# Attention on one Trainium2 core: the values product of a 512-query step in one piece instead of two

## The reference, cut to what matters

```
def _attn(x, wq, wk, wv, wo, bq, bk, bv, bo):
    q, k, v = ...                               # 16 heads of 8 dimensions
    att = jnp.einsum('bhqd,bhkd->bhqk', q, k) * hd ** (-0.5)
    att = jnp.where(causal, att, -jnp.inf)
    att = jax.nn.softmax(att, axis=-1)
    y = jnp.einsum('bhqk,bhkd->bhqd', att, v)
    return y.transpose(...).reshape(Bb, T, C) @ wo + bo
```

## Time and profile before

| | us |
|---|---|
| median of 3 runs | 3347.49 (3345.98 to 3355.19) |
| the profiled execution | 3349.13 |
| its span in the profile | 3347.4 |
| the 512-query groups 4 to 7 of one causal layer | 73.2 |
| all 24 groups of one causal layer, 903 to 1275 | 372 |

### The profile page before, as it was taken

One profiled execution on the slowest core, in us unless ns is written; L12 is line 12 of the kernel. 1 busy time (PEld: TensorE's weight loads), 2 busy tenths in 40 slices (PEclk: granted clock), 3 DMA queues, 4 the chain that ended last, 5 costly groups with the idle time before them and its releaser, 6 DMA issues. The chain is left out here.

```text
span 3347.4 us, 75365 instructions
## 1 busy us (share of the span) xinstructions
PE 2748.5 (82%) x29824; PEld 1299.9 (39%) x29824; DVE 2337.0 (70%) x3203; ACT 2171.7 (65%) x4160; POOL 331.7 (10%) x868
## 2 busy tenths in 40 slices
PE   4459999699499994859999998389996996799967
PEld 3322332599333332612222222233333995233326
DVE  5659997322499993469999996499993223799953
ACT  1137889354278983339999998168884453588853
POOL 3023110000031100000000000031100000221000
PEclk8669999799699997969999999699997998799988
DMA  2060000000500001140000000600001003200010
GB/s 56 7 142 27 13 11 8 30 0 0 126 21 15 10 10 45 40 88 8 10 8 10 8 8 25 138 18 16 12 10 32 1 0 75 65 18 11 10 34 25
DMA packets 96737, 99.80 MB, mean 30 GB/s; under 512 B 13158, under 2 KB 84644, under 8 KB 96420
## 3 DMA queue, kind: packets, MB, share of 16 engines
q1 hardware_dynamic: 79140, 77.62, 8.8%
q10 hardware_dynamic: 16640, 15.73, 1.9%
q0 software_dynamic: 640, 2.10, 0.2%
HBM read 51.44 MB, written 43.65 MB: 28 GB/s over the span
## 5 line engine op out<-in xcount | busy, mean ns | idle before, releaser
L1189 ACT ACTIVATE h_probsf<-h_ps_scoresf 128x512 f32<-128x512 f32 (+3 forms) x1216 | 603.5, 552 | 155.3 <-PE h_ps_scoresf L1141 142.9
L1189 ACT ACTIVATE h_probsg<-h_ps_scoresg 128x512 f32<-128x512 f32 (+3 forms) x1216 | 603.6, 552 | 150.8 <-PE h_ps_scoresg L1141 138.3
L1189 ACT ACTIVATE h_probsb<-h_ps_scoresb 128x512 f32<-128x512 f32 x1024 | 556.3, 596 | 73.8 <-PE h_ps_scoresb L1141 63.8
L1163 PE MATMUL h_ps_valuesf<-h_probsf,v_all 128*9 128x256 f32 (+2 forms) x4608 | 348.8, 375 | 29.5 <-POOL h_probsf L1252 21.9
L1163 PE MATMUL h_ps_valuesg<-h_probsg,v_all 128*9 128x256 f32 (+2 forms) x4608 | 347.5, 374 | 26.3 <-POOL h_probsg L1252 18.6
L1163 PE MATMUL h_ps_valuesb<-h_probsb,v_all 128*9 128x256 f32 x4096 | 318.4, 383 | 9.4 <-ACT h_drainedb L1196 4.8
L1212 DVE TENSOR_REDUCE h_maxima_0b<-h_ps_scanb 128x2 f32<-128x1024 f32 x256 | 292.5, 1217 | 10.9 <-PE h_ps_scanb L1103 9.6
L1212 DVE TENSOR_REDUCE h_maxima_2b<-h_ps_scanb 128x2 f32<-128x1024 f32 x256 | 292.8, 1217 | 6.7 <-PE h_ps_scanb L1103 6.7
L1103 PE MATMUL h_ps_scanf<-k_stack,q_stack 48*128 48x512 bf16 (+3 forms) x1280 | 218.1, 363 | 69.9 <-DVE h_ps_valuesf L1201 51.5
L1212 DVE TENSOR_REDUCE h_maxima_0f<-h_ps_scanf 128x2 f32<-128x1024 f32 x224 | 259.2, 1219 | 22.6 <-PE h_ps_scanf L1103 22.3
L1103 PE MATMUL h_ps_scang<-k_stack,q_stack 48*128 48x512 bf16 (+3 forms) x1280 | 217.0, 361 | 70.3 <-DVE h_ps_valuesg L1201 50.4
(11 more groups left out here) (423 smaller groups left out, 3865.9 us busy)
## 6 DMA issues: line engine op xcount, KB each, us to landing
q_stack<-q_parts ACTq DMA_DIRECT2D x20, 256.0 KB, 8.3
k_stack<-k_parts ACTq DMA_DIRECT2D x20, 256.0 KB, 9.8
q_stack<-q_parts SPq DMA_DIRECT2D x20, 256.0 KB, 8.8
k_stack<-k_parts SPq DMA_DIRECT2D x20, 256.0 KB, 10.7
attended<-h_drainedf SPq DMA_DIRECT2D x16, 256.0 KB, 2.3
attended<-h_drainedf SPq DMA_DIRECT2D x32, 128.0 KB, 1.9
attended<-h_drainedb SPq DMA_DIRECT2D x32, 128.0 KB, 1.9
attended<-h_drainedg SPq DMA_DIRECT2D x16, 256.0 KB, 2.2
```

Of the source, the lines that this page charges most:

```text
L1163: last = nc.tensor.matmul(ps_values[32 * j:32 * j + VD, low:high], m.v_all[:, kb, QUAD * quad + j, :], probs[:, (u + j % banks) % RING_P, ...
L1189: nc.scalar.activation(by_head(probs[:, of % RING_P, :], of), by_head(ps_scores[:, of % RING_S, :], of), ACT.Exp, scale=SOFTMAX_SCALE).the ...
```

## The change

`halves` gives one piece for every step, whatever its width:

```
@@ class Plan, def halves(self, n_step) @@
         high = self.queries(self.steps[n_step][0])
         width = high - self.offsets[n_step]
-        n = 2 if width > CH // 2 else 1
-        return [(high - width + h * width // n, high - width + (h + 1) * width // n) for h in range(n)]
+        return [(high - width, high)]
```

## The result

The changed kernel is slower: median 3401.12 us (3400.59 to 3407.52, four runs) against 3346.73 before, ratio 1.0162 with a 95% interval of 1.0141 to 1.0183. The forecast was 3383 with a range of 3340 to 3410. The direction and the mechanism were right, and the place in the main; the size was 54 us where I had 36. The 3401 measured lies nearer to the 3406 of the clock rival than to the forecast.

A forecast was written before the change was run, and what follows sets the result against it. PE, DVE and ACT's loop were taken to bound groups 4 to 7 together. Terms of 1.2, 3.0, 2.1, 0.4, 1.8 and 0.5 gave 9.0 us a layer, 36 in four: 3383 us (median), chance 0.60, range 3340 to 3410.

The forecast's parts named there:

- the clock rival: Thinner PE work makes the granted clock fall twice more a layer, 2.9 us each, +23 us: 3406 us; chance 0.12.
- Three limits within 6%: Groups 4 to 7 bound at once by ACT's loop 1.07, PE's cycle 1.09 and DVE's scan 1.13 us.
- The piece left, 1.00 us: One values piece of 512 columns holds PE 1.00 us, bounded by 0.90 and 1.12; ends worth -10 to +12 us.
- The spacing, 1.07 and 1.53 us, a step of 2.60: Plain-scan steps: score gap without values 1.07 us (ACT's loop), with values 1.53 (PE's work); step 2.60, before 2.18 or 2.27.
- Third scans: A second scan placed in the hole makes the next scan wait for DVE, up to 0.6 us; together +1.8 us a layer.
- Groups 4 to 7, 8.5 us a layer: Losses in groups 4 to 7 of each causal layer: 1.2, 3.0, 2.1, 0.4 and 1.8 us; 80 to 83 us for 73.2.
- The diagonal steps: Steps with diagonal scans go from 2.54 to 2.78 us, +0.24 on PE's terms; 5 of a group's 13 scans are diagonal.
- Groups 0 to 3, 0.5 us a layer: Group 0 loses nothing; groups 1 to 3 lose 3 x 0.35 x 0.5 = 0.5 us, part hidden by waits for scan buffers.
- Groups 8 to 23, 0: These groups keep their pieces and start from the same state, so they keep their time: 0.
- Faster through less PE work: Rival: 6.7 us a layer of PE work comes off, DVE caps it at 5.2, 21 in all: 3327 us; chance 0.13.
- DVE decides: Rival: both scans of a step fit the hole, group time is that of its scans, no change: 3350 us; chance 0.15.

The follow-up runs named there:

- the filled changed kernel: Changed kernel plus extra 0.22 us scans into a free buffer at the ends of groups 1 and 7 and the change from 22 to 23: 1.0114, median 3385.34 us.

## Why the prediction was right, and where its size was off

- *Three limits within 6%.* Borne out for ACT's loop: shorter exponentials gain the kernel before 0.28%. For DVE no run tested it in the kernel before.
- *The piece left, 1.00 us.* Measured 0.98. Its width costs nothing else (the run with two products in one turn).
- *The spacing, 1.07 and 1.53 us, a step of 2.60.* Measured 1.07 and 1.52, 2.59; shorter exponentials move the first to 0.86 and not the second.
- *Third scans.* They are there, with a wait of 0.47 us each. I had 1.8 us a layer. Without them (the old order with one piece) groups 5 and 6 are 0.5 and 0.6 us shorter at the full clock, and the kernel 0.3%, about 10 us or 2.6 a layer, part of which may be the clock.
- *Groups 4 to 7, 8.5 us a layer.* Measured 8.0 in the two profiled executions, and 9.0 with both kernels at the full clock. The two differ in group 4. I counted 1.2 us for it, and at the full clock it is 1.2 (19.6 against 18.4). The profiled executions show nothing (20.7 against 21.0) because the fall in group 4 lasts 3.4 us after the change in the two middle layers and 6.8 before: the changed kernel got back some 1.5 us there, which I had not foreseen. The diagonal steps had 0.4 to 0.5 a group; they cost nothing that shows in groups 4 and 5, and 0.7 each in groups 6 and 7.
- *Groups 0 to 3, 0.5 us a layer.* About right for the work: 0.7 at an unchanged clock (29.3 against 28.6), all in group 1. Groups 2 and 3 show none of it; in group 3, where DVE is busy 10.17 of 10.70 us, DVE would hide it whole and not by half, though no run tested that. The rest of the 1.9 to 3.3 us in the table is falls of the clock.
- *Groups 8 to 23, 0.* The orders are the same from group 8 on, as I said, but the layers lost 0.7 to 4.3 us to falls of the clock there, 8.4 in all. With those stretches filled all four take 247.2 at a clock of 1.00.
- *The clock rival* had 0.12, as a case apart. It came about together with the forecast. The step that failed is that I priced falls at 0 in the sum, though the row with a fall after 1.92 us of work in 3.40 stood beside a step that leaves PE idle a quarter of the time. By the filled changed kernel that term is 16 us: 38 for the work and 16 for the falls are the 54 measured. That the range held 3401 is owed to its width, and not to a price for the clock in the sum. The price I did name, 2.9 us a fall, was too high as well, since it compared group 4 with group 5: group 4 against itself without the fall is 21.0 against 18.4, 2.6.
- *Faster through less PE work:* PE's busy time did fall by 1.9 us in groups 4 to 7 (66.43 for 68.31) and the groups took longer all the same. *DVE decides:* refuted by groups 5 and 6 with shorter maxima, which fall by only 0.5 us each.

The 16 us are measured for the filled kernel as a whole. How they divide between layers was seen in one profiled execution only, and falls move between executions.

## What to carry to other kernels

When PE, DVE and ACT are within a few per cent of each other, as here, the length of PE's longest uninterrupted piece can matter more than the sum of its work. It has to fit inside the loop that feeds the next engine, here 1.07 us for a ring of three score banks, of which 0.53 is already spoken for by scores and scan. A piece of 256 columns (0.56 us) just fits, one of 512 (0.98) doesn't. Compare each piece with that loop, before counting what is saved on fixed costs. And a change that opens holes in PE's stream should be priced at both clock levels; a group whose clock differs between two profiles is compared at equal clock before its difference is given a cause.

## What the runs showed of the hardware that I had not expected

The granted clock fell after stretches in which PE never idled longer than 0.8 us at once, with 1.89, 1.92, 2.02 and 2.29 us of work in 3.40. It stayed up over others of that kind, as at the change from group 22 to 23 in three of four layers of the kernel before. Which of the thin stretches has a fall differed between layers and with small edits: filling the one before group 4 removed its fall in four layers of four and left groups 8 to 23 some 1.9 us longer in three. A fall removed from one profiled execution is therefore no gain until the median says so.

Four float32 products in 32-column strips hold PE the same whether issued as one set of 512 columns (0.98 us) or as two of 256 back to back (0.99). Two pieces of 256 with scores and a scan between them hold it 0.56 us each, 1.12. So the fixed 0.12 us of a piece is paid on entering values from other work, not for each instruction, beside the 0.09 us that a scan before values holds PE longer.
